# Key search of an attention and mixture-of-experts kernel: GpSimd writes shifted copies of the keys, and one VectorE instruction with accumulator delivers the base of the next round

## The reference, cut to what matters

```python
x = x + xattn(layernorm(x), ctx_1024, ctx_1024, Wq, bq, Wk, bk, Wv, bv)
# the second part, on layernorm(x):
S = jax.nn.sigmoid(xt @ Wg).T                 # (8 experts, 4096 tokens)
G, I = jax.lax.top_k(S, k)                    # k = 1024 for each expert
ex = xt[I]
hid = gelu(einsum('ekh,ehf->ekf', ex, W1) + b1[:, None, :])
out = (einsum('ekf,efh->ekh', hid, W2) + b2[:, None, :]) * G[..., None]
new_x = zeros_like(xt).at[I.reshape(-1)].add(out.reshape(-1, h))
```

## Time and profile before

| | |
|---|---|
| time, median of 3 runs | 593.31 us (592.85 to 594.45) |
| the profiled execution: its time, its span | 593.0 us, 591.0 us |
| mean granted TensorE clock | 0.944 of full |
| phase A | to about 173 us of the span |
| the 15 rounds | 174.75 to 200.23 us |
| rest of the selection, to the first matmul of expert 0 | to 223.11 us |
| eight experts | to the end |

### The profile page before, as it was taken

One profiled execution on the slowest core, in us unless ns is written; L12 is line 12 of the kernel. 1 busy time (PEld: TensorE's weight loads), 2 busy tenths in 40 slices (PEclk: granted clock), 3 DMA queues, 4 the chain that ended last, 5 costly groups with the idle time before them and its releaser, 6 DMA issues.

```text
span 591.0 us, 11403 instructions
## 1 busy us (share of the span) xinstructions
PE 533.8 (90%) x3894; PEld 384.1 (65%) x3895; DVE 372.9 (63%) x956; ACT 344.6 (58%) x622; POOL 252.3 (43%) x463
## 2 busy tenths in 40 slices
PE   3999999999863328999999999999999999999995
PEld 2676778877751125596497497487487488487484
DVE  3688887777678855764773763763763863852821
ACT  4468666786463205934944944953952952963931
POOL 2435543342140040554554554455455355366045
PEclk9999999999775558999999999999999999999999
DMA  8782232221241010443345335335326336244024
GB/s 212 236 284 74 72 108 79 98 74 36 98 96 65 1 55 19 137 105 49 124 76 90 125 60 101 117 57 112 107 55 124 87 74 118 63 101 52 9 27 46
DMA packets 46647, 53.54 MB, mean 91 GB/s; under 512 B 7380, under 2 KB 42520, under 8 KB 46616
## 3 DMA queue, kind: packets, MB, share of 16 engines
q1 hardware_dynamic: 34328, 36.09, 19.2%
q0 software_dynamic: 12288, 17.05, 17.5%
HBM read 36.22 MB, written 16.91 MB: 90 GB/s over the span
## 4 chain that ended last, share of the span: by engine, by line
PE 79%; issue 7%; DVE 7%; POOL 3%; ACT 2%; DMA 1%; POOLq 0%; ACTq 0%; DVEq 0%
PE bank L895 67%; PE bank L1085 3%; PE bank L1075 3%; PE bank L915 2%; DVE junk L665 2%; PE bank L987 2%; POOL out L374 2%; PE bank L902 2%; DMA out<-yo,ids_s 1%; POOL ex L361 1%; DVE thr L686 1%; PE bank L1051 1%; DMA ex<-rows_d,ids 0%; ACT xn L399 0%; DVE oneh L776 0%
## 5 line engine op out<-in xcount | busy, mean ns | idle before, releaser
L895 PE MATMUL bank<-w2h,xres 128*128 128x256 f16 x1024 | 173.6, 273 | 0.0
L895 PE MATMUL bank<-w2l,xres 128*128 128x256 f16 x512 | 139.6, 273 | 0.0
L840 DVE TENSOR_TENSOR xres<-g,xres 128x512 f16<-128x512 f32 x128 | 87.6, 689 | 60.9 <-ACT xres L506 60.9
L374 POOL DMA_INDIRECT out<-yo,ids_s x64 | 100.1, 1563 | 27.3 <-issue 26.2
L895 PEld LDWEIGHTS bank<-w2h,xres 128*128 128x128 f16 x1024 | 100.1, 98 | 12.2
L502 ACT ACTIVATE g<-bank,b1e 128x512 f32<-128x512 f32 x128 | 88.0, 688 | 25.1 <-PE bank L895 20.0
L519 ACT ACTIVATE yo<-yt,ge 128x256 f32<-128x256 f32 x64 | 32.5, 508 | 118.2 <-DVE yt L854 118.2
L895 PE MATMUL bank<-exTh,w1h 128*128 128x512 f16 x256 | 97.5, 381 | 1.5 <-DVE exTl L824 1.5
L895 PE MATMUL bank<-exTl,w1h 128*128 128x512 f16 x256 | 97.6, 381 | 0.0
L895 PE MATMUL bank<-exTh,w1l 128*128 128x512 f16 x256 | 97.6, 381 | 0.0
L506 ACT ACTIVATE xres<-bank,b1e 128x512 f16<-128x512 f32 x128 | 87.2, 681 | 0.0
(11 more groups left out here) (187 smaller groups left out, 965.8 us busy)
## 6 DMA issues: line engine op xcount, KB each, us to landing
w1r<-in_L_ffn_W SPq DMA_DIRECT2D x8, 1024.0 KB, 6.0
w2r<-in_L_ffn_W SPq DMA_DIRECT2D x8, 1024.0 KB, 5.7
ctx<-in_ctx SPq DMA_DIRECT2D x8, 512.0 KB, 3.6
out<-xres SPq DMA_DIRECT2D x8, 512.0 KB, 3.0
rows_d<-xn SPq DMA_DIRECT2D x8, 512.0 KB, 3.0
xres<-in_x SPq DMA_DIRECT2D x1, 3072.0 KB, 18.3
xres<-in_x SPq DMA_DIRECT2D x2, 512.0 KB, 4.8
b_bc<-in_L_ffn_b SPq DMA_DIRECT2D x8, 128.0 KB, 3.6
```

Source lines behind the costliest of these rows:

```text
L374: pool.indirect_dma_start(out=rows_out, out_offset=bass.IndirectOffsetOnAxis(ap=ids_s[:, t:t + 1], axis=0), in_=yo[:, t, :], in_offset=Non ...
L840: dve.tensor_tensor(hid[1][:, f, h * 512:(h + 1) * 512], g32[:, u % 2, :], hid[0][:, f, h * 512:(h + 1) * 512], ALU.subtract).then_inc(s[" ...
L895: last = pe.matmul(out, lhs(a, c), rhs(b, c), start=i == 0, stop=i == len(terms) - 1)
```

## The change

Thresholds are no longer moved; the keys are. For each round but the first of each half, GpSimd writes three copies of the keys, lowered by one, two and three steps (the third also raised by a half, for the signs). All three counts then compare with one number, the base, which is the fourth column of `gain[:, r]`. The copies go to `kshift`, two sets of three, which lie in the memory of `yo`, a tile of the experts that is unused until then. GpSimd may write the set of round r when the counts of round r - 2 are done.

The sums of a round now have a fourth column that always passes (128 times 16 is above 1024). `gain[:, r]` holds three times the step and the base. One instruction compares the four sums with 1024 and multiplies with `gain`; its accumulator is the new base, written into the next round's `gain`, or to `t12` after the last round of a half. `thr`, `offs`, `digit`, `move`, `ahead` and the memsets of the thresholds are gone. The signs are taken of base minus key, so `half16` becomes `nhalf16`.

```diff
+        gain = sb("gain", [P, ROUNDS, 4])
+        third = sb("third", [P, 2])
+        passed = sb("passed", [P, 4])
...
+        kshift = yo[:].rearrange("p t d -> p (t d)")[:, 0:6 * 2 * P].rearrange("p (r j a k) -> p r j a k", r=2, j=3, a=2)
...
+            def shifted_keys(keys, r):
+
+                if r >= 2:
+                    pool.wait_ge(s["srch_cmp"], 2 * (r - 1))
+                    pool.wait_ge(s["srch_act"], r - 1)
+                for j in range(3):
+                    pool.tensor_scalar(kshift[:, r % 2, j], keys[:], 0.5 * (j == 2) - (j + 1) * STEP[r], None, ALU.add).then_inc(s["shift_s"], 1)
+
+            pool.wait_ge(s["khi_s"], 1)
+            for r in range(1, HI_ROUNDS):
+                shifted_keys(khi, r)
+            pool.wait_ge(s["krel2_s"], 1)
+            for r in range(HI_ROUNDS + 1, ROUNDS):
+                shifted_keys(krel, r)
...
             for r in range(ROUNDS):
-                act.wait_ge(s["thr_s"], r + 1)
+                phase, first = r // HI_ROUNDS, r in (0, HI_ROUNDS)
...
+                else:
+                    act.wait_ge(s["shift_s"], 3 * (r - phase))
+                    act.wait_ge(s["base_s"], r)
...
-                count_pair(keys, r)
-                dve.wait_ge(s["thr_s"], r + 1)
-                dve.scalar_tensor_tensor(offs[:], sgn[:], thr[:, 3:4], ahead[:, r, :], ALU.mult, ALU.add).then_inc(s["offs_s"], 1)
+                first = r in (0, HI_ROUNDS)
+                if r:
+                    dve.wait_ge(s["base_s"], r)
+                for j in range(2):
+                    if not first:
+                        dve.wait_ge(s["shift_s"], 3 * (r - 1 - r // HI_ROUNDS) + j + 1)
+                    dve.tensor_scalar(junk[:, j], keys[:] if first else kshift[:, r % 2, j], (j + 1) * STEP[r] if first else gain[:, r, 3:4],
+                                      None, ALU.is_ge, ALU.add, accum_out=cnt[:, j:j + 1]).then_inc(s["srch_cmp"], 1)
                 dve.wait_ge(s["srch_mm"], r + 1)
-                dve.tensor_scalar(passed[:], A_[:, 1, 0:3], float(K), None, ALU.is_ge, ALU.add,
-                                  accum_out=digit[:]).then_inc(s["digit_s"], 1)
-                dve.wait_ge(s["digit_s"], r + 1)
-                dve.wait_ge(s["offs_s"], r + 1)
-                if last is None:
-                    dve.scalar_tensor_tensor(thr[:], move[:, r, :], digit[:, 0:1], offs[:], ALU.mult, ALU.add).then_inc(s["thr_s"], 1)
...
+                dve.scalar_tensor_tensor(passed[:], A_[:, 1, 0:4], float(K), gain[:, r, :], ALU.is_ge, ALU.mult,
+                                         accum_out=found).then_inc(s["base_s"], 1)
...
-                pe.matmul(A_[:, 1, 2:3], same16[:], c128[:], start=True, stop=False, skip_group_check=True)
+                pe.matmul(A_[:, 1, 2:4], same16[:], c128[:], start=True, stop=False, skip_group_check=True)
```

More of the change, by code:

```diff
@@ L131, in build @@
         asign = sb("asign", [P, 2, P], BF16)
[L132 to L140, removed]
+        nhalf16 = sb("nhalf16", [P, P], BF16)
+        c128 = sb("c128", [P, 2], BF16)
+        gain = sb("gain", [P, ROUNDS, 4])
+        third = sb("third", [P, 2])
+        passed = sb("passed", [P, 4])
         t12 = sb("t12", [P, 2]); t12i = sb("t12i", [P, 2], I32); tshl = sb("tshl", [P, 1], I32); kthi = sb("kthi", [P, 1], I32)
@@ L330, in body @@
                 if k in (2, NP - 2):
-                    pool.memset(sgn[:, 0:4:2] if k == 2 else sgn[:, 1:4:2], 1.0)
                     for r in range(ROUNDS):
                         if (r < HI_ROUNDS) == (k == 2):
[L335 to L342, removed]
+                            pool.memset(gain[:, r, 0:3], STEP[r])
+                            if r in (0, HI_ROUNDS):
+                                pool.memset(gain[:, r, 3:4], 0.0)
+                                pool.memset(third[:, r // HI_ROUNDS:r // HI_ROUNDS + 1], 3.0 * STEP[r] - 0.5)
                     if k == NP - 2:
@@ L475, in _ @@
             for r in range(ROUNDS):
-                act.wait_ge(s["thr_s"], r + 1)
+                phase, first = r // HI_ROUNDS, r in (0, HI_ROUNDS)
                 if r == 0:
+                    act.wait_ge(s["srch_c"], 1)
                     act.wait_ge(s["khi_s"], 1)
-                if r == HI_ROUNDS:
+                elif first:
                     act.wait_ge(s["krel2_s"], 1)
+                    act.wait_ge(s["srch_mm"], r)
+                else:
+                    act.wait_ge(s["shift_s"], 3 * (r - phase))
+                    act.wait_ge(s["base_s"], r)
                 with nc.allow_low_precision(reason="sums of 256 signs are whole numbers of at most 256"):
-                    act.activation(asign[:], khi[:] if r < HI_ROUNDS else krel[:], ACT.Sign, bias=thr[:, 2:3],
+                    act.activation(asign[:], (krel if phase else khi)[:] if first else kshift[:, r % 2, 2], ACT.Sign, scale=-1.0,
+                                   bias=third[:, phase:phase + 1] if first else gain[:, r, 3:4],
                                    accum_out=cnt[:, 2:3]).then_inc(s["srch_act"], 1)
@@ L659, in _ @@
             phase_a(dve, body)
[L662 to L673, removed]
@@ L690, in _ @@
             dve.wait_ge(s["srch_c"], 1)
-            dve.memset(sgn[:, 2:3], -1.0)
-            first_thresholds(0)
             dve.wait_ge(s["key_ev"], 1)
@@ L699, in _ @@
             dve.wait_ge(s["khi_s"], 1)
-            dve.wait_ge(s["thr_s"], 1)
             for r in range(HI_ROUNDS):
-                search_round(khi, r, t12[:, 0:1] if r == HI_ROUNDS - 1 else None)
+                search_round(khi, r, t12[:, 0:1] if r == HI_ROUNDS - 1 else gain[:, r + 1, 3:4])
                 if r == 0:
@@ L715, in _ @@
             dve.wait_ge(s["krel2_s"], 1)
-            dve.wait_ge(s["thr_s"], HI_ROUNDS + 1)
             for r in range(HI_ROUNDS, ROUNDS):
[L718 to L721, removed]
+                search_round(krel, r, t12[:, 1:2] if r == ROUNDS - 1 else gain[:, r + 1, 3:4])
+            dve.wait_ge(s["base_s"], ROUNDS)
             dve.tensor_copy(t12i[:], t12[:]).then_inc(s["t12i_s"], 1)
```

18 lines of the change are left out of this document (6 added, 12 removed).

## The result

The changed kernel takes 605.99 us (604.81 to 607.69, 4 runs), against 593.08 us before (591.61 to 594.45, 4 runs). The ratio is 1.0223, 95% interval 1.0204 to 1.0241: 12.9 us slower. The forecast was 590.5, 2.8 us faster, with a range up to 594.5. The direction was wrong. Of the four rivals it is the second, GpSimd slower than the chain, and beyond the upper end that was given for it.

What follows compares the result with a forecast made beforehand. TensorE, 90% busy, bounds the whole program, but the search is a chain of waits: 15 rounds save 3.0 us, the cast loses 0.2, so -2.8 from the 593.31 median gives 590.5 us; 8-in-10 range 589.0 to 594.5.

Steps and rivals of the forecast that it cites:

- the second, GpSimd slower than the chain: In the search, GpSimd copies of 0.57 to 0.73 us set the pace: change +0.6 to +6.9 us, about 597.1; chance 0.12.
- The place: The search, 174.75 to 200.23 us: 15 rounds of 1.64 us through VectorE and TensorE; a round's gain moves everything behind.
- What goes from the chain: Between compare and next counts in each search round, threshold writing (L686, L688) goes: 0.47 us becomes 0.21.
- The new compare: VectorE's four-column compare with accumulator in each search round: 0 to 0.13 us added, 0.06 taken.
- The failed step: GpSimd's 256-column copies in the search: 0.37 us each from affine selects, upper end 0.73 from a two-input row.
- The formula: Search paced by GpSimd copies of T us each: total change 39 T - 21.6 us, zero at T = 0.554.
- The range: Whole-kernel time: forecast's own range 589.0 to 592.0 us; for 8 in 10, 589.0 to 594.5.
- The first: In the search, GpSimd copies of 0.48 to 0.57 us set the pace: -2.8 to +0.6, about 592.2 us; chance 0.13.
- The third: VectorE's 26 search counts each wait 0.18 us on average for GpSimd copies: 4.8 us, 595.3; chance 0.06.
- The fourth: In the search compare, the accumulator's way into `gain` costs as much as L686: -0 to -1 us, 592.8; chance 0.05.
- The cast of `klo`: VectorE's cast at L705, behind the first compare, waits for GpSimd copies: 0 to 1.0 us, 0.2 taken.
- The clock: TensorE's clock rise after expert 0 starts: follows the work's start, no change taken, about 1 us kept either way.

## Why the prediction was wrong, point by point

- **The place.** Right: the search is a loop of its own, and the spans differ by 12.5 us where it grew by 12.4.
- **What goes from the chain.** Right: 0.26 a round. The two kernels whose GpSimd copies fit into the round, and the one without such copies, have rounds of 1.38 to 1.39 us and are 3.9 to 4.3 us faster than before.
- **The new compare.** It costs nothing (162 against 163 ns), the lower end; 0.06 was taken.
- **The failed step: "I take 0.37: the copies have one input, as the affine selects do, and nothing needs a second read."** A copy has one input and costs 0.85, spaced 0.89 on average (18.77 us for the first 21, 173.07 to 191.84). The number of inputs does not order GpSimd's forms: 2.5 ns a column for the tensor_scalar, 0.61 us in all for two inputs, 0.40 for a plain copy. The affine select stood in for the tensor_scalar, and the two-input row was called the upper end without a reason that excludes more. The affine select itself takes 0.40 at 256 columns, so its extrapolation was nearly right; it was the wrong row. The tensor_scalar's 0.85 lies 0.12 above the upper end.
- **The formula.** 39 T - 21.6 held to 0.7 us. With 0.89 it gives +13.1, and the search grew by 12.4. With 0.57 it gives +0.6, and the search of that kernel grew by 0.03. About half of the 0.7 is in the ends of the halves: from ScalarE's start to the compare it took 0.92 (191.86 to 192.78) and 0.91, where the sum had 1.11. Where VectorE's pace gives way to GpSimd's has only been bracketed: 1.14 us of copies a round (two of 0.57) left the round at 1.38, 1.71 us of copies did not.
- **The range.** The ends given for the forecast's own range, 589.0 and 592.0, do not follow from their terms: 3.9 and 1 off 593.3 give 588.4, and 1.95 less 0.35 with 1 from the clock give 592.7. The wider range for 8 in 10 cut off most of the second rival, which is where the measured time lay, and beyond.
- **The rivals.** The second had the mechanism, a chance of 0.12 and an upper end of +6.9. The first had the same mechanism with a smaller size. The third, counts that collide, is refuted for this kernel: 26 counts of 478 ns. The fourth is refuted by the read 0.09 behind the compare. The page GPSIMD Engine Reference of the Trainium skill, Engine selection, has a one-input operation at roughly line rate; that fits the copy (0.40, where VectorE's cast of the same size takes 0.29) and not the tensor_scalar. The page's 2.6 cycles a column (section Elementwise — side-by-side cycle accounting), which the prediction set beside the second rival, are its figure for a tensor_tensor. An estimate from them at the page's 1.2 GHz, with the 140 ns of the earlier trace rows, is 256 x 2.2 + 140 ns = 0.70 us; the tensor_tensor took 0.61 and the tensor_scalar 0.85.
- **The cast of `klo`.** 0.2 taken. It took 0.34 in place of 0.29 and lay under GpSimd's copies; beside tensor_tensor copies it took 0.74.
- **The clock.** The rise came 4.5 us later behind the work's start than before. That is 2.2 us by the estimate above, twice the 1 us that was kept for it. A search that began 1.65 earlier made up for it, by luck: the kernels built on the changed one began theirs anywhere from 173.03 to 175.48.

What stays open: which part of a GpSimd instruction holds a two-input VectorE instruction. Beside tensor_scalar copies a count grew by 0.05 us on average, beside tensor_tensor copies by 0.29; that is what the runs show, not why. Open too is why the tensor_scalar is GpSimd's dearest form by the column; the runs give its price and not the reason.

## What to carry to other kernels

Before work is moved to an idle engine, time that very instruction there, in its form and size; a row of another form on the same engine does not bound it, even if it has as many inputs. If a helper's work per round exceeds the round, its time replaces the chain's, whatever the chain has saved: here 3 x 0.89 replaced 1.64. A cheaper form (tensor_tensor for tensor_scalar) took the loss of 12.9 us away; with a third of the load on another engine besides, the same idea was 4 us faster. An idle test load can cost more than the effect that it is to show: of the 3.8 us that it added to one trace here, 1.45 lay in the loop under study, and the rest behind it.

## What the runs showed of the hardware that was not expected

- On GpSimd, adding a constant by tensor_scalar costs more (0.85 us for 128x256 f32) than adding a broadcast column by tensor_tensor (0.61).
- Of VectorE's instructions beside GpSimd's work, the tensor_scalar count with accumulator never grew (475 to 478 ns in every kernel that has it), the two-input count grew from 482 ns to 534 or 774 by GpSimd's form, and the cast of `klo`, 0.29 alone, took 0.34 to 0.42 beside tensor_scalar copies and 0.74 beside tensor_tensor copies. The Trainium skill's page SBUF — State Buffer, Who interferes with whom, excepts the accumulator form and names the other two, and the runs agree; its statement that the loser waits for the whole instruction does not fit a growth of 0.05 us beside tensor_scalar copies of 0.85; the 0.29 beside tensor_tensor copies do not contradict it.
- On VectorE a count whose threshold is an immediate (a number in the instruction) took 413 ns; with a pointer to a column of numbers it took 475 on the same tile.
